# Two graph attention layers: the attention is drained from PSUM by ScalarE, and GpSimd keeps only the normaliser

## What is computed

```python
h = maximum(layernorm(x), 0)
Wh = h @ W                                  # 1024 x 128
e = Wh @ a1 [:, None] + Wh @ a2 [None, :]   # 1024 x 1024
e = where(e > 0, e, 0.2 * e)
attention = softmax(where(adj > 0, e, -9e15), axis=2)
x = x + elu(attention @ Wh)                 # layer 1: x + attention @ Wh
```

## Time and profile before

| | |
|---|---|
| device time, median of 3 runs | 339.63 us |
| span of the profiled execution | 337.6 us |
| PE busy | 303.5 us (90%) |
| DVE busy | 294.8 us (87%) |
| ACT busy | 122.1 us (36%) |
| POOL busy | 119.5 us (35%) |
| mean granted TensorE clock | 0.973 |
| accumulator taken, stage 9, 10 and 11 | 199.56, 218.16 and 238.04 us |

### The profile page before, as it was taken

One profiled execution on the slowest core, in us unless ns is written; L12 is line 12 of the kernel. 1 busy time (PEld: TensorE's weight loads), 2 busy tenths in 40 slices (PEclk: granted clock), 3 DMA queues, 4 the chain that ended last, 5 costly groups with the idle time before them and its releaser, 6 DMA issues.

```text
span 337.6 us, 6932 instructions
## 1 busy us (share of the span) xinstructions
PE 303.5 (90%) x2567; PEld 297.0 (88%) x2567; DVE 294.8 (87%) x610; ACT 122.1 (36%) x356; POOL 119.5 (35%) x71
## 2 busy tenths in 40 slices
PE   6979798999897999979998899979999799798975
PEld 6879797998896999969998899969999799798975
DVE  5687599799999899998799899998999988956895
ACT  1773143244450535334441444524351354313000
POOL 3330027252326624164244624056243612441330
PEclk9999979799999999989999999999999799979999
DMA  7983938015680375515762365504761300103011
GB/s 231 408 328 102 372 151 307 5 65 154 222 278 35 127 245 180 201 44 162 233 228 83 125 204 167 188 0 153 254 224 58 120 7 11 54 0 117 12 62 62
DMA packets 15239, 50.45 MB, mean 149 GB/s; under 512 B 2040, under 2 KB 3056, under 8 KB 15216
## 3 DMA queue, kind: packets, MB, share of 16 engines
q1 hardware_dynamic: 15216, 50.14, 42.9%
HBM read 45.88 MB, written 4.26 MB: 148 GB/s over the span
## 4 chain that ended last, share of the span: by engine, by line
DVE 45%; PE 33%; issue 8%; DMA 5%; ACT 4%; POOL 2%; DVEq 1%; SPq 1%; ACTq 0%
DVE pbuf L527 22%; PE acc L737 22%; PE prj L691 5%; DVE zrow L508 4%; DVE accs L544 3%; DVE stats L469 3%; DMA row_r<-r_rows 3%; DVE ex L560 3%; PE tp L683 3%; DVE x L567 3%; ACT xn L387 2%; PE acc L755 2%; POOL rstd L322 2%; DVE cmax L506 1%; DMA r_rows<-rT 1%
## 5 line engine op out<-in xcount | busy, mean ns | idle before, releaser
L737 PE MATMUL acc<-wh,pbuf 128*128 128x129 f32 x1984 | 238.9, 281 | 4.9 <-DVE accs L544 3.7
L737 PEld LDWEIGHTS acc<-wh,pbuf 128*128 128x128 f32 x1984 | 234.0, 197 | 5.7 <-issue 5.4
L527 DVE SCALAR_TENSOR_TENSOR pbuf<-row_r,sqr,adj_sb 128x1024 f32<-128x1024 f32 x127 | 177.3, 1443 | 16.5 <-DMA row_r<-r_rows 16.5
L345 POOL TENSOR_TENSOR hp<-accs,rec 128x1024 f32<-128x1024 f32 x15 | 29.3, 1956 | 134.8 <-DVE rec L554 134.8
L322 POOL TENSOR_TENSOR rstd<-vareps,neg_half 128x8 f32<-128x8 f32 x16 | 38.8, 2423 | 66.5 <-DVE vareps L489 63.0
L387 ACT ACTIVATE xn<-x,shift,rstd 128x128 f32<-128x128 f32 (+1 forms) x123 | 49.0, 480 | 0.0
L408 ACT ACTIVATE wh<-prj,wh 128x128 f32<-128x128 f32 x128 | 35.9, 359 | 0.5
L691 PE MATMUL prj<-w_ext,hT 128*128 128x130 f32 x256 | 31.4, 276 | 0.4 <-ACT hT L394 0.4
L691 PEld LDWEIGHTS prj<-w_ext,hT 128*128 128x128 f32 x256 | 30.1, 192 | 0.6 <-issue 0.6
L469 DVE BATCH_NORM_STATS2 stats<-x 128x6 f32<-128x128 f32 (+1 forms) x128 | 26.2, 278 | 4.0 <-issue 3.9
L544 DVE TENSOR_TENSOR accs<-acc,uniform 128x387 f32<-128x387 f32 (+1 forms) x48 | 22.3, 506 | 5.5 <-PE acc L737 3.1
(11 more groups left out here) (51 smaller groups left out, 153.1 us busy)
## 6 DMA issues: line engine op xcount, KB each, us to landing
adj_sb<-in_adj SPq DMA_DIRECT2D x64, 512.0 KB, 5.0
row_r<-r_rows SPq DMA_DIRECT2D x15, 512.0 KB, 4.1
x<-in_x SPq DMA_DIRECT2D x7, 512.0 KB, 4.7
out_x<-x SPq DMA_DIRECT2D x7, 512.0 KB, 2.9
x<-in_x SPq DMA_DIRECT2D x2, 256.0 KB, 2.8
out_x<-x SPq DMA_DIRECT2D x2, 192.0 KB, 1.9
r_rows<-rT SPq DMA_DIRECT2D x15, 4.0 KB
w_ext<-in_w SPq DMA_DIRECT2D x2, 64.0 KB, 3.0
```

The lines of the kernel that those rows point to most:

```text
L345: nc.gpsimd.tensor_tensor(hp[:, :, :], accs[:, :, 0:D], rec[:, :].unsqueeze(2).to_broadcast([P, T, D]), ALU.mult).then_inc(hp_ready, 1)
L527: nc.vector.scalar_tensor_tensor(pbuf[:, t, :], row_r[:, g, :], sqr[:, g, 0, t:t + 1], adj_at(b, t), ALU.max, ALU.min).then_inc(p_ready, 1)
L737: mm = nc.tensor.matmul(acc[:, k, s * C:(s + 1) * C], pbuf[:, t, i * P:(i + 1) * P], wh[:, g, t, :], start=(t == 0 and s == 0), stop=(t == ...
```

## The change

ScalarE takes the attention out of PSUM itself. VectorE now only inverts the denominators, in place in PSUM, one instruction for each bank (`invert`). ScalarE then scales each of the eight tiles by its `rec` into `hp` (`drain`), and writes the uniform row into the emptied bank as the start value of the next stage (`seed`), so all matmuls of a stage accumulate (`start=False`). For that TensorE's accumulate bits must be set once, which eight plus two plus two matmuls of 387 columns do at the start (`set_bits`) in place of 42 short transposes. The elu's second part is rewritten: ScalarE makes relu(1 - exp(hp)), VectorE max(hp, 0) minus that (`add_hp`), and then adds x0 (`add_x0`). In layer 1 VectorE adds hp to x1. GpSimd loses L332, L345 and L350. `turn_r` moves behind tile 2. The store waits for VectorE's `add_hp` rather than for GpSimd.

```diff
-    WARM = (24, 10, 8, 8, 10)
+    WARM = (8, 2, 2, 8, 10)
...
+        def stage_of_layer1(b):
+            return LAST - 1 if isinstance(b, int) and b == B - 2 else 2 * b + 3
...
             def store(b):
-                sp.wait_ge(out_ready, b + 1)
+                sp.wait_ge(hp_free, stage_of_layer1(b) + 1)
...
-            def epilogue(e, l, b):
...
-                nc.gpsimd.tensor_tensor(hp[:, :, :], accs[:, :, 0:D],
...
+            def drain(e, g):
+                if not (isinstance(e, int) and e == 0):
+                    act.wait_ge(hp_free, e)
+                for t, (k, s) in enumerate(bank_of):
+                    if s == 0:
+                        act.wait_ge(rec_ready, NB * e + k + 1)
+                    op = nc.scalar.activation(hp[:, t, :], acc[:, k, s * C:s * C + D], ACT.Copy,
+                                              scale=rec[:, t:t + 1])
+                    if s == tiles_in[k] - 1:
+                        op.then_inc(acc_drained, 1)
+                    if k > 0 and s == 0:
+                        reseed(e, g, k - 1)
+                reseed(e, g, NB - 1)
+            def reseed(e, g, k):
+                act.wait_ge(acc_drained, NB * e + k + 1)
+                seed(g, k)
+            def seed(g, k):
+                w = tiles_in[k]
+                nc.scalar.activation(acc[:, k, 0:w * C].rearrange("p (s c) -> p s c", c=C),
+                                     uniform[:, g, :].unsqueeze(1).to_broadcast([P, w, C]),
+                                     ACT.Copy).then_inc(acc_seeded, 1)
...
+                act.wait_ge(ex_ready, b + 1)
+                nc.scalar.activation(ex[:, :], ex[:, :], ACT.Relu, bias=1.0,
+                                     scale=-1.0).then_inc(elu_ready, 1)
...
             def stage(n, g, l, b, epi, prep, norm):
-                if epi is not None and epi[0] == 0:
-                    elu_exp(n - 1, epi[1])
+                if epi is not None:
+                    drain(n - 1, g)
+                    if epi[0] == 0:
+                        elu_exp(n - 1, epi[1])
...
-            def copy_acc(e, g, k):
...
+            def invert(e, k):
                 dve.wait_ge(acc_done, NB * e + k + 1)
                 w = tiles_in[k]
+                den = acc[:, k, 0:w * C].rearrange("p (s c) -> p s c", c=C)[:, :, D]
+                nc.vector.reciprocal(rec[:, k * NB:k * NB + w], den).then_inc(rec_ready, 1)
...
+            def add_hp(e, l, b):
+                hp_row = hp[:, :, :].rearrange("p t d -> p (t d)")
+                if l == 0:
+                    dve.wait_ge(elu_ready, b + 1)
...
+                    nc.vector.scalar_tensor_tensor(x_at(x1, b), hp_row, 0.0, ex[:, :], ALU.max,
+                                                   ALU.subtract).then_inc(hp_free, 1)
+                else:
+                    dve.wait_ge(acc_drained, NB * e + NB)
+                    nc.vector.tensor_tensor(x_at(x1, b), hp_row, x_at(x1, b),
+                                            ALU.add).then_inc(hp_free, 1)
+            def add_x0(e, l, b):
+                if l == 0:
+                    dve.wait_ge(hp_free, e + 1)
+                    nc.vector.tensor_tensor(x_at(x1, b), x_at(x1, b), x_at(x0, b),
+                                            ALU.add).then_inc(x1_ready, 1)
...
                     layernorm()
                     masks(5)
-                    elu(elu_half)
+                    residual(add_hp)
                     masks(6)
-                    elu(elu_rest)
+                    residual(add_x0)
                     masks(7)
...
-                    if t == 0 and s == 0 and not (isinstance(n, int) and n == 0):
-                        pe.wait_ge(acc_copied, NB * (n - 1) + k + 1)
+                    if t == 0 and s == 0:
+                        pe.wait_ge(acc_seeded, NB * n + k + 1)
...
-                    tiles(1)
+                    tiles(1, 2)
                     turn_r(n + 1, 1 - g)
-                    tiles(2, 3, 4, 5, 6)
+                    tiles(3, 4, 5, 6)
```

More of the change, by code:

```diff
@@ L427, in rows @@
             def rows(m, g):
-                before = 2 if isinstance(m, int) and m == 0 else 4
                 exps(m, g)
-                scale_wh(m, g, range(before))
-                copy_r(m, g)
-                scale_wh(m, g, range(before, T))
+                if isinstance(m, int) and m == 0:
+                    scale_wh(m, g, range(2))
+                    copy_r(m, g)
+                    act.wait_ge(bits_set, 1)
+                    act.wait_ge(e_copied, 3)
+                    seed(g, 0)
+                    scale_wh(m, g, range(2, 4))
+                    seed(g, 1)
+                    seed(g, 2)
+                else:
+                    scale_wh(m, g, range(4))
+                    copy_r(m, g)
@@ L434, in setup @@
+                scale_wh(m, g, range(4, T))
             def setup():
@@ L601, in masks, with residual @@
                         mask(n, g, l, b, t)
-                def elu(*parts):
-                    if epi is not None and epi[0] == 0:
+                def residual(*parts):
+                    if epi is not None:
                         for part in parts:
-                            part(epi[1])
+                            part(n - 1, *epi)
                 def layernorm():
@@ L629, in stage @@
                     masks(0, 1)
-                    take_acc(n - 1, 1 - g)
-                    masks(*range(2, T))
+                    take_acc(n - 1)
+                    masks(2, 3, 4)
+                    residual(add_hp)
+                    masks(5, 6, 7)
                     return
                 masks(*range(TAKE_AFTER + 1))
-                take_acc(n - 1, 1 - g)
+                take_acc(n - 1)
                 prep_e()
@@ L638, in stage @@
                 if norm_is_late(n):
-                    elu(elu_half, elu_rest)
+                    residual(add_hp, add_x0)
                     layernorm()
@@ L716, in turn_r, with set_bits @@
                                     ident[:, :]).then_inc(r_turned, 1)
+            def set_bits(count):
+                for k in ([*range(NB)] * count)[:count]:
+                    mm = nc.tensor.matmul(acc[:, k, 0:NB * C], ident[:, :],
+                                          ident[:, 0:1].to_broadcast([P, NB * C]), start=True,
+                                          stop=True, skip_group_check=True)
+                return mm
             def keep_warm(count):
                 for _ in range(count):
-                    nc.tensor.transpose(acc[:, 0, 0:P], ident[:, :], ident[:, :])
+                    nc.tensor.transpose(tp[:, BANK:BANK + P], ident[:, :], ident[:, :])
             def attend(n, g, t):
@@ L761, in setup @@
             def setup():
-                pe.wait_ge(const_set, 5)
-                keep_warm(WARM[0])
+                pe.wait_ge(const_set, 4)
+                set_bits(WARM[0])
                 pe.wait_ge(w_in, 96)
@@ L768, in setup @@
                 mm.then_inc(wa_done, 1)
-                keep_warm(WARM[1])
+                set_bits(WARM[1])
                 transposes(0)
-                keep_warm(WARM[2])
+                set_bits(WARM[2]).then_inc(bits_set, 1)
                 pe.wait_ge(wext_ready, 1)
```

87 lines of the change are left out of this document (19 added, 68 removed).

## The result

The changed kernel takes 344.33 us (median of 20 runs, 339.79 to 347.76) against 339.82 us of the kernel before (20 runs, 337.57 to 342.40). The ratio is 1.009, with a 95% interval of 1.006 to 1.012: a little slower.

What follows compares the result with a forecast made beforehand. VectorE was taken to bound A stages, VectorE then the row's DMA B stages. Terms sum to -0.5 us, slow tiles make +1.8: 337.6 becomes 339.4, plus 2.0 for the median gives 341.4; own range 338 to 345, 8 in 10 333 to 348.

Steps and rivals of the forecast that it cites:

- GpSimd lengthens VectorE's work: On VectorE beside GpSimd, the mask behind R takes 2.60 us against 1.28, zrow 2.02 against 0.23.
- The gain on mask 4 ends ahead of `cmax`: Blocked mask 4 gives back 1.3 us on VectorE, which then idles 1.3 us ahead of cmax in each stage.
- R to c is 4.6 us: From VectorE taking the accumulator (R) to cmax's start (c): drains and seeds make 4.6 us, before 4.57; bounds 4.1, 5.4.
- B: the store holds the row: Even stages 4 to 12 (B): row issued behind the waiting store; VectorE waits 2.5 us; 0.3 longer, five times +1.5.
- A stays at 18.6: Odd stages 3 to 11 (A): row lands just when mask 7 ends; each stays at 18.6 us, term +0.
- Two slow tiles of five: TensorE's tile 0 at low clock after two of five stalls: 1.5 us each, +3.0 less 0.7 for present slow ones.
- The rival of all pairs going slow: Slower: every pair of stages slow at tile 0, from four pairs on +3 to +4.5 more, 345 to 347 us; 20%.
- Start and end: Start +1.0 (-0.6 to +4), stage 1 +0.5, stage 2 -1.5, stage 14 -0.6, last stage -1.7 us.

Runs made afterwards that it cites:

- e7: Changed kernel, with GpSimd multiplying two spare 128x1024 arrays in each stage once the reciprocals are there: 342.85 us, ratio 1.010 to the kernel before.
- e4: Changed kernel without the seeds (uniform row left out of the computation, tile 0's first matmul of each bank overwrites): 323.29 us, ratio 0.946 to the kernel before.
- e11: e3 without the seeds (uniform row left out of the computation, first matmul of a bank overwrites): 311.13 us, ratio 0.917 to the kernel before.
- e2: Changed kernel with the store moved behind the spread of the row in SyncE's queue: 333.47 us, ratio 0.976 to the kernel before.
- e5: Changed kernel with 16 (odd stages) or 8 (even) short transposes on TensorE between project and tile 0: 340.15 us, ratio 1.002 to the kernel before.
- e1: The changed kernel run again without an edit, as base for the other runs: 345.17 us, ratio 1.014 to the kernel before.
- e9: Kernel before with one part of the change alone, turn_r behind tile 2: 338.96 us, ratio 0.997 to the kernel before.
- e3: Changed kernel with the store behind the spread of the row and turn_r back behind tile 1: 320.61 us, ratio 0.942 to the kernel before.
- e6: Changed kernel with turn_r back behind tile 1 alone, store left in place: 339.80 us, ratio 0.998 to the kernel before.
- e12: e3 with the third bank drained and seeded by VectorE instead of ScalarE: 321.65 us, ratio 0.948 to the kernel before.

## Why the prediction was right, point by point

The time came out 2.9 us above the forecast of 341.4, inside its own range, and on the side that it leaned to. The change itself was forecast at +1.8 us and came to +4.5 in the medians. The waits were the ones forecast; the sizes of some were not.

- **GpSimd lengthens VectorE's work.** Right. Masks take 1.28 us throughout (mean 1279 ns in the page, 1443 before), `zrow` 232 ns (889 before); e7 brings the long mask back with GpSimd. For `zrow` and the masks of B no run puts GpSimd back.
- **The gain on mask 4 ends ahead of `cmax`.** Right, and shown by e7: the contention can be put back for nothing. VectorE ends mask 4 sooner than I had it, at R+2.1 in stage 9 and R+2.7 in stage 10 and not at R+3.3, so that with the copies gone, too, it idles 1.86 us in stage 10 and 3.68 in stage 9 (1.2 of it the slow tile 0), for 1.3 forecast.
- **R to c is 4.6 us.** 4.55 to 4.61 in the stages 3 to 12 wherever the clock is full. The single prices: seeds of 387 elements 525 ns (0.53 from the line through two other sizes), of 258 elements 392 ns (0.42), drains every 0.265 us. The estimate of 0.29 us a drain from the Trainium skill ("ScalarE: Activation LUTs", "What ACT_TABLE_LOAD costs") would have put c at R+4.8; the rows of L408 were the better source. e4 and e11 show that the seeds in this chain count: 1.1 us off R to c, in the stages 3 to 13 in e4 and nearly in B alone in e11, and 21.9 and 9.5 us off the total.
- **B: the store holds the row.** Right in each number: store at c+5.8, row at c+6.2 (I had c+6.3), next R at c+15.43 (15.55). e2 shows it as a cause. I gave 2.5 us of wait for the row in B; it is 2.47 to 2.76. TensorE's waits for the first two seeds are 1.97 and 0.25 us behind this stall, for 2.5 forecast, and 1.02 and 0.25 in the other kind, for 1.
- **A stays at 18.6.** Here the sum was short. The row's DMA was issued at c+5.2 to c+5.6 (I had c+5.2) and landed 4.2 to 4.7 us after that, not 4.1, and A is 18.8 and 19.1 even where the clock is full (stages 3 and 5). My 4.1 was the shortest of the five such landings in B of the kernel before; the others took 4.2 to 4.6. I had the row arriving "just when mask 7 ends", which left no room for that. Whether the adjacency tiles that are loaded beside it add to it is not shown. In stage 9 it waits 0.83 us (218.80 in the trace), partly because slow tiles delay `turn_r`, too.
- **Two slow tiles of five.** Mis-sized. Three of the five A stages, and stage 13, had one; each cost 1.2 us between R and c, as forecast, but with the later row these A stages grew by 1.3 to 2.1 us. That is the largest miss: +6.3 us in A where I had +2.3 (+3.0 less 0.7). The rival of all pairs going slow asked for four of five; the kernel lies between the two, and by the rival's own price (+3 to +4.5 on 341.4) it would have read 344.4 to 345.9, not 345 to 347, so the time alone does not tell it from my forecast. e5 settles the cause.
- **Start and end.** The start came to +0.9 (I had +1.0), and that was luck: in e1 it is -0.9, in six more executions with these start matmuls (e2 to e7) R of stage 1 lies between 41.26 and 42.30, and the kernel before, with another place for `turn_r` (e9), has it at 42.72. No run shows that the start costs anything at R of stage 1. The weights' matmul itself was later than I thought (9.90 in place of 9.05), since the slow pace lasted for more of the long matmuls. Stage 1 +1.0 for +0.5, stage 2 -1.5, stage 14 -1.6 for -0.6. The last stage gave nothing where I had -1.7: TensorE stalled 1.82 us for the first seed and then ran its tiles 0 and 1 at 0.51 of the clock, which I had counted only for the pairs. In e3, where that stall is 1.19 us and the clock stays at 1.00, it gave 1.4 us.

The clock of the last stage of the changed kernel, by windows (columns as above):

```profile
322.00:325.00 3.00, 1.18 (x9) 0.84 (x7) 3.00 (x7) 2.56 (x9) 0.00 (x0) 1.00 0.01 3
325.00:328.00 3.00, 2.81 (x14) 2.79 (x14) 3.00 (x3) 0.84 (x3) 0.00 (x0) 0.51 0.00 0
```

What stays open is which stalls the low clock follows. In the changed kernel TensorE stalls 1.88 to 1.99 us ahead of tile 0 in stages 5, 7, 9, 11 and 13 (only 0.37 in stage 3); the clock stayed full in stage 5 and fell in the other four. In e1 it is the same five stages and the same one spared, with a stall of 2.09 us. In e6 stalls of 1.7 to 2.2 us were followed by the low clock twice in five. So the number of slow tiles can differ between executions, and the 20 runs of the changed kernel, each with its mean clock on record, spread with it: 339.8 to 343.2 us at 0.975, 340.4 to 344.6 at 0.970, 344.3 to 345.8 at 0.965, 347.8 at 0.961.

## What to carry to other kernels

When work is taken off a busy engine, look at what that engine waits for next before counting the gain: here 44 us of VectorE's time bought nothing until a store and one small transpose were moved in two queues, and then bought 6%. In a queue that holds several transfers, a wait of one is a wait of all behind it; when the producer of the first changes, ask when each of the others will go out. And a stall of the matrix engine on the critical path can cost more than its length, if the clock falls and the work behind it is what the others wait for.

## What the runs showed of the hardware

- A stall of TensorE of 1.9 to 2.0 us ahead of the first bank (in stage 9 1.97, and 0.25 more ahead of the second: 1.06 us busy in a window of 3) was followed by a granted clock of 0.50 to 0.57 in four stages of five, and in e2, where that wait is 0.65 to 0.99 us, in none of the stages 4 to 13. Sixteen transposes of the identity (1.91 us) in the gap kept it at 1.00.
- GpSimd's pass over 128x1024 with both operands in SBUF, 2.35 us in e7, lengthened the VectorE mask beside it by 0.4 to 1.8 us there. In the kernel before, `zrow`, with 8 elements, took 1.8 us longer beside GpSimd's addition to x1.
- ScalarE writes a seed of 387 elements into PSUM in 525 ns, no less than the 527 ns of the line through its copies of other sizes; VectorE's copy of 258 elements (e12) takes 430 ns against ScalarE's 392.
- At the start the eight matmuls of 387 columns (16 instructions) took 8.44 us: 0.64 us from one to the next for about 6 us, where I had let the slow stretch end after 4 us; four later ones took 1.47 us. In e1 the sixteen took 7.75 us. The profile's granted clock reads 1.00 in both stretches, so that this is the clock is inferred from the pace alone.
